# The last quantised product of a feed-forward block: magnitudes with a running maximum, and the signed product formed in the down stage

## What is computed

```python
def act_qdq(x):                       # one scale for the whole tensor
    scale = jnp.maximum(jnp.max(jnp.abs(x)) / 32767, 1e-12)
    return jnp.clip(jnp.round(x / scale), -32768, 32767) * scale
...
x = act_qdq(x)
up = act_qdq(x @ lpbq_dequant(w_up).T)
gate = act_qdq(x @ lpbq_dequant(w_gate).T)
sig = fixed_qdq_u16(jax.nn.sigmoid(gate))
gate = act_qdq(gate * sig)
o = act_qdq(gate * up)
return o @ lpbq_dequant(w_down).T
```

## Time and profile before

| | us |
|---|---|
| median of 3 runs (1158.4 to 1158.91) | 1158.68 |
| the profiled execution's own time | 1158.46 |
| its span in the trace | 1156.7 |
| last 74.7 us: product stage and its scale steps | 33.1 |
| down stage to the start of PE's second group | 8.95 |
| from there to the end | 32.65 |

### The profile page before, as it was taken

The page is one execution under the profiler, slowest core; times in us unless marked ns, Lnnn a source line. Parts: engine busy times, 40 slices in busy tenths (PEclk is TensorE's granted clock), DMA queues, the critical chain, the costliest instruction groups (busy, mean ns, idle before and its releaser), DMA issues.

```text
span 1156.7 us, 20436 instructions
## 1 busy us (share of the span) xinstructions
PE 1075.9 (93%) x8326; PEld 500.6 (43%) x8326; DVE 1006.6 (87%) x1390; ACT 604.5 (52%) x705; POOL 37.2 (3%) x41
## 2 busy tenths in 40 slices
PE   5999999999999999999999999999999998999059
PEld 3443344434443444344434443444343322887049
DVE  7687988898889889998999899987989999849995
ACT  3555555555555555545454555454555464449652
POOL 0500000000000000000000000000000000003200
PEclk9999999999999999999999999999999999999579
DMA  8001300010001000100010001000100000000002
GB/s 273 8 20 25 119 20 20 20 38 20 20 20 38 20 19 20 38 20 20 20 38 20 20 20 38 20 19 20 29 20 19 20 29 10 1 1 0 0 1 74
DMA packets 37860, 34.57 MB, mean 30 GB/s; under 512 B 14209, under 2 KB 28738, under 8 KB 37510
## 3 DMA queue, kind: packets, MB, share of 16 engines
q1 hardware_dynamic: 37766, 33.26, 9.3%
HBM read 30.75 MB, written 2.36 MB: 29 GB/s over the span
## 4 chain that ended last, share of the span: by engine, by line
PE 63%; DVE 24%; issue 6%; ACT 6%; DMA 0%; POOL 0%; POOLq 0%; DVEq 0%; ACTq 0%
PE ps L1345 20%; PE ps L1361 20%; DVE acc L906 9%; DVE e_buf L1000 6%; PE ps L1221 4%; PE ps L1273 3%; PE ps L1493 3%; PE ps L1231 3%; PE ps L1239 3%; PE ps L1538 3%; ACT e_buf L651 2%; PE ps L1250 1%; DVE gt L1148 1%; ACT z L732 1%; ACT z L734 1%
## 5 line engine op out<-in xcount | busy, mean ns | idle before, releaser
L651 ACT ACTIVATE e_buf<-ps 128x1024 f32<-128x1024 f32 x400 | 410.6, 1027 | 311.2 <-PE ps L1345 311.2
L1361 PE MATMUL ps<-e_buf,vb 64*64 64x512 f32 x3072 | 402.4, 594 | 7.0 <-DVE e_buf L1000 6.9
L906 DVE TENSOR_TENSOR acc<-acc,e_buf 128x1024 f32<-128x1024 f32 x320 | 388.8, 1215 | 0.0
L1000 DVE TENSOR_SCALAR e_buf<-e_buf 128x1024 f32<-128x1024 f32 x400 | 272.9, 682 | 71.3 <-ACT e_buf L651 70.1
L1361 PEld LDWEIGHTS ps<-e_buf,vb 64*64 64x64 f32 x3072 | 111.8, 133 | 225.7 <-issue 194.1
L1345 PE MATMUL ps<-qb,kb_odd 64*64 64x512 f32 x1600 | 208.7, 589 | 0.0
L1345 PE MATMUL ps<-qb,kb_even 64*64 64x512 f32 x1600 | 208.6, 589 | 0.0
L1345 PEld LDWEIGHTS ps<-qb,kb_odd 64*64 64x64 f32 x1600 | 61.6, 133 | 109.8 <-issue 109.5
L1345 PEld LDWEIGHTS ps<-qb,kb_even 64*64 64x64 f32 x1600 | 61.3, 133 | 110.2 <-issue 110.1
L1493 PE MATMUL ps<-hT,wgu 128*128 128x512 f32 x288 | 67.7, 396 | 0.1
L989 DVE TENSOR_TENSOR xacc<-ps,xacc 128x512 f32<-128x512 f32 x60 | 40.5, 687 | 27.2 <-PE ps L1273 26.7
(11 more groups left out here) (145 smaller groups left out, 770.9 us busy)
## 6 DMA issues: line engine op xcount, KB each, us to landing
ebc<-el_rows SPq DMA_DIRECT2D x64, 128.0 KB, 2.9
rden<-inv_rows SPq DMA_DIRECT2D x62, 128.0 KB, 2.9
xacc<-in_x_dram SPq DMA_DIRECT2D x4, 512.0 KB, 7.1
wst<-in_L_xattn_Wkv_dram SPq DMA_DIRECT2D x16, 128.0 KB, 2.8
out_dram<-z SPq DMA_DIRECT2D x7, 256.0 KB, 2.1
wst<-in_L_xattn_Wq_dram SPq DMA_DIRECT2D x8, 128.0 KB, 2.8
wo_raw<-in_L_xattn_Wo_dram SPq DMA_DIRECT2D x8, 128.0 KB, 2.9
acc<-in_ctx_dram SPq DMA_DIRECT2D x2, 512.0 KB, 7.2
```

The lines of the kernel that those rows point to most:

```text
L651: nc.scalar.activation(e_buf[:, g % E_BUFS, :, :], sc[:, g % 2, :, :], ACT.Exp, scale=float(DH) ** -0.5).then_inc(exp_done, 1)
L906: dve.tensor_tensor(acc[:, t0 % 3, :, :], a, e_buf[:, tiles_to(t0, st) % E_BUFS, :, :], ALU.add).then_inc(summed, 1)
L1000: dve.tensor_scalar(tile, tile, EXP_LO, EXP_HI, ALU.max, ALU.min).then_inc(clip_done, 1)
L1361: ins = pe.matmul(ps_o[DH * h:DH * h + DH, half, :], vb[rows, p % 2, st, DH * h:DH * h + DH], e_buf[rows, g % E_BUFS, h, :], start=(st == ...
```

## The change

For half of the chunks (`MAGS`: 2, 3, 6, 7, 10, 11) ACT writes the magnitudes of both rounded factors, and DVE multiplies them and keeps a running maximum in one instruction, `tensor_tensor_reduce`. For the other half (`SIGNED`: 0, 1, 4, 5, 8, 9) DVE multiplies the signed factors and reduces the product with `top` as before, now into and out of a scratch tile `om` that both kinds of chunk share, each step waiting for the one before. No product is kept: the down stage forms it again from the int16 factors, rounded in the same instruction (`scalar_tensor_tensor`). ACT makes the int16 gate of each group for that (`gate_integers`), and POOL makes all twelve chunks of the int16 `ui`, the six signed ones first. The gate integers have four buffers, and `ohl` moves into the memory of the gate and up weights. PE's program isn't touched.

```diff
--- before.py
+++ after.py
@@ -52,6 +52,10 @@
 FC = 2 * NB
 FCH = FT * N // FC
 GROUPS = NT // 2
+GQ_BUFS = 4
+MAGS = [e for e in range(FCH) if e % NBS >= 2]
+SIGNED = [e for e in range(FCH) if e % NBS < 2]
+POOL_UI = SIGNED + MAGS
 
 
 def rows_of(st):
@@ -278,14 +282,17 @@
                 hT = sb("hT", [P, 2, KT, N], F32R, stack=first)
                 up = sb("up", [P, FT, N], stack=first)
             ui = sb("ui", [P, FT, N], I16, stack=ffn)
-            sb("pad2", [P, (2 * KT * N - FT * N // 2)], stack=ffn)
-            ohl = sb("ohl", [P, 2, 2, FT, DM], F32R, stack=ffn)
             oi = sb("oi", [P, 2, FT, DM], I16, stack=ffn)
+            gs_i = sb("gs_i", [P, 2, FT, DM], I16, stack=ffn)
         zf = z[:, :, :].rearrange("p t d -> p (t d)")
         hi16 = zf[:, 0:N].bitcast(I16)
         sg = zf[:, 0:2 * FC].rearrange("p (a f n) -> p a f n", a=2, f=2)
         gi = zf[:, 2 * FC:3 * FC].bitcast(I16).rearrange("p (a f n) -> p a f n", a=2, f=2)
         su = zf[:, 3 * FC:4 * FC].bitcast(U16T).rearrange("p (a f n) -> p a f n", a=2, f=2)
+        gq = zf[:, 0:2 * FC].bitcast(I16).rearrange("p (a f n) -> p a f n", a=GQ_BUFS, f=2)
+        um = zf[:, 2 * FC:3 * FC].bitcast(I16).rearrange("p (a f n) -> p a f n", a=2, f=2)
+        om = zf[:, 3 * FC:4 * FC].rearrange("p (f n) -> p f n", f=2)
+        ohl = wgu[:, :, :, :, :].rearrange("p a b k f -> p (a b k f)").rearrange("p (a i f d) -> p a i f d", a=2, i=2, f=FT)
         wpiece = [zf[:, FF * n:FF * n + FF] for n in range(5)] + [wdown1[:, :]]
 
         psum = nc.psum_tensor("ps", [P, 8, NB], F32)
@@ -319,7 +326,8 @@
         scale_done = sem("scale_done")
         f1_ready, f1_out = sem("f1_ready"), sem("f1_out")
         gi_done, sig_done, su_done = sem("gi_done"), sem("sig_done"), sem("su_done")
-        gs_done, gq_done, ui_done, ui_pool, o_done = sem("gs_done"), sem("gq_done"), sem("ui_done"), sem("ui_pool"), sem("o_done")
+        gs_done, gq_done, ui_pool, o_written, o_done = sem("gs_done"), sem("gq_done"), sem("ui_pool"), sem("o_written"), sem("o_done")
+        um_done, gs_ready = sem("um_done"), sem("gs_ready")
         oi_done, o_high, o_low = sem("oi_done"), sem("o_high"), sem("o_low")
         f2_ready, f2_out, stored = sem("f2_ready"), sem("f2_out"), sem("stored")
 
@@ -367,10 +375,7 @@
 
         def await_ui(eng, e):
 
-            if e < 2:
-                eng.wait_ge(ui_pool, e + 1)
-            else:
-                eng.wait_ge(ui_done, e - 1)
+            eng.wait_ge(ui_pool, POOL_UI.index(e) + 1)
 
 
         @block.sync
@@ -540,7 +545,7 @@
                     pool.wait_ge(gs_done, e - 1)
                 pool.tensor_scalar(su[:, e % 2, :, :], sg[:, e % 2, :, :], U16, 1.0, ALU.mult, ALU.mult).then_inc(su_done, 1)
             pool.wait_ge(scale_done, 3)
-            for e in range(2):
+            for e in POOL_UI:
                 pool.tensor_scalar(chunk(ui, e), chunk(up, e), fsc[:, 2, 2:3], 1.0, ALU.mult, ALU.mult).then_inc(ui_pool, 1)
 
 
@@ -734,19 +739,34 @@
                 nc.scalar.activation(sg[:, e % 2, :, :], gi[:, e % 2, :, :], ACT.Sigmoid, scale=fsc[:, 1, 1:2]).then_inc(sig_done, 1)
             act.wait_ge(scale_done, 3)
             for e in range(FCH):
-                if e >= 2:
-                    nc.scalar.activation(chunk(ui, e), chunk(up, e), ACT.Copy, scale=fsc[:, 2, 2:3]).then_inc(ui_done, 1)
-                    act.wait_ge(o_done, e - 1)
-                nc.scalar.activation(gi[:, e % 2, :, :], chunk(gt, e), ACT.Copy, scale=fsc[:, 3, 2:3]).then_inc(gq_done, 1)
+                if e >= GQ_BUFS:
+                    act.wait_ge(o_done, e - GQ_BUFS + 1)
+                nc.scalar.activation(gq[:, e % GQ_BUFS, :, :], chunk(gt, e), ACT.Abs if e in MAGS else ACT.Copy,
+                                     scale=fsc[:, 3, 2:3]).then_inc(gq_done, 1)
+                if e in MAGS:
+                    nc.scalar.activation(um[:, e % 2, :, :], chunk(up, e), ACT.Abs, scale=fsc[:, 2, 2:3]).then_inc(um_done, 1)
+
+            def gate_integers(g):
+
+                if g >= 2:
+                    act.wait_ge(oi_done, g)
+                nc.scalar.activation(gs_i[:, g % 2, :, :], gt[:, :, DM * g:DM * g + DM], ACT.Copy, scale=fsc[:, 3, 2:3]).then_inc(gs_ready, 1)
+
+            act.wait_ge(ui_pool, len(SIGNED))
+            for g in range(2):
+                gate_integers(g)
             for m in range(2):
                 act.wait_ge(oi_done, m + 1)
                 nc.scalar.copy(ohl[:, 0, 0, :, P * m:P * m + P], oi[:, 0, :, P * m:P * m + P]).then_inc(o_high, 1)
+            gate_integers(2)
             for g in range(1, GROUPS):
                 act.wait_ge(oi_done, g + 2)
                 if g >= 2:
 
                     act.wait_ge(f2_ready, g - 1)
                 nc.scalar.copy(ohl[:, g % 2, 0, :, :], oi[:, g % 2, :, :]).then_inc(o_high, 1)
+                if g + 2 < GROUPS:
+                    gate_integers(g + 2)
 
 
         @block.vector
@@ -1142,15 +1162,23 @@
             link(top(fst[:, 3, pieces - 2:pieces], chunk(gt, FCH - 1)))
             scale_of(2, 2, pieces, 2)
             link(dve.tensor_tensor(pre[:, 4:5], fsc[:, 3, 1:2], fsc[:, 2, 1:2], ALU.mult))
+            dve.memset(fst[:, 4, :], 0.0)
             for e in range(FCH):
                 dve.wait_ge(gq_done, e + 1)
-                await_ui(dve, e)
-                dve.tensor_tensor(chunk(gt, e), gi[:, e % 2, :, :], chunk(ui, e), ALU.mult).then_inc(o_done, 1)
-                if e >= 1:
-                    dve.wait_ge(o_done, e)
-                    top(fst[:, 4, 2 * e - 2:2 * e], chunk(gt, e - 1))
+                if e in MAGS:
+                    dve.wait_ge(um_done, MAGS.index(e) + 1)
+                    if e:
+                        dve.wait_ge(o_done, e)
+                    dve.tensor_tensor_reduce(om, gq[:, e % GQ_BUFS, :, :], um[:, e % 2, :, :], 1.0, 0.0, ALU.mult, ALU.max,
+                                             fst[:, 4, 2 * e:2 * e + 1]).then_inc(o_done, 1)
+                else:
+                    await_ui(dve, e)
+                    if e:
+                        dve.wait_ge(o_done, e)
+                    dve.tensor_tensor(om, gq[:, e % GQ_BUFS, :, :], chunk(ui, e), ALU.mult).then_inc(o_written, 1)
+                    dve.wait_ge(o_written, SIGNED.index(e) + 1)
+                    top(fst[:, 4, 2 * e:2 * e + 2], om).then_inc(o_done, 1)
             dve.wait_ge(o_done, FCH)
-            link(top(fst[:, 4, pieces - 2:pieces], chunk(gt, FCH - 1)))
             scale_of(4, 1, pieces, 3)
             link(dve.tensor_tensor(fsc[:, 4, 3:4], fsc[:, 4, 1:2], tg[:, 1:2], ALU.mult))
 
@@ -1159,8 +1187,11 @@
 
                     dve.wait_ge(o_high, g)
                     dve.wait_ge(o_low, g - 1)
-                dve.tensor_scalar(oi[:, g % 2, :, r0:r1], gt[:, :, DM * g + r0:DM * g + r1], fsc[:, 4, 2:3], None,
-                                  ALU.mult).then_inc(oi_done, 1)
+                dve.wait_ge(gs_ready, g + 1)
+                if g == GROUPS // 2 and r0 == 0:
+                    dve.wait_ge(ui_pool, FCH)
+                dve.scalar_tensor_tensor(out=oi[:, g % 2, :, r0:r1], in0=gs_i[:, g % 2, :, r0:r1], scalar=fsc[:, 4, 2:3],
+                                         in1=ui[:, :, DM * g + r0:DM * g + r1], op0=ALU.mult, op1=ALU.mult).then_inc(oi_done, 1)
 
             def out_low(g):
                 dve.wait_ge(o_high, g + 2)
```

## The result

The changed kernel takes 1166.57 us (median of 4 runs, 1165.6 to 1167.08) against 1158.76 for the kernel before (4 runs). The ratio is 1.0066, 95% interval 1.0054 to 1.0078: 7.8 us slower. The forecast was slower, by 4.3 us; the upper end of its range, 1166.5, is 7.8 us above the 1158.68 that it started from, so the result lies just at that end.

A forecast was written before the change was run, and what follows sets the result against it. DVE was taken to bound the product stage and PE the down stage. Product stage -0.3, PE's queue +2.5 and down stage +2.2 made 4.4 us on 1158.46, giving 1163.0 us; range 1158.3 to 1166.5.

The forecast's parts named there:

- POOL's exclusion: Product stage: two-tensor DVE operations and POOL instructions exclude each other; 4.6 to 4.7 us waiting; rival without it 0.13.
- the two take turns: Product stage: DVE and POOL alternate when both always have work; a POOL that loses a turn moves 0.7 us.
- The fused maximum: Product stage, magnitude chunks: one `tensor_tensor_reduce` at 1.31 us, 1.35 with gap; dear rival 2.3 to 2.46, chance 0.14.
- PE's queue: Before the down stage: spreading matmuls queue behind nine idle matmuls that start later; adds 2.5 us.
- The rounding: Down stage: two-tensor int16 `scalar_tensor_tensor` takes 1.83 us for 1,536 columns, 1.01 for a half of group 0.
- the second mark: Spreading matmuls to PE's second down group: forecast 2.2 us longer, from the dearer rounding on DVE.
- The rule of half rate: Down stage rival: rounding with two non-bf16 SBUF sources at half rate, near 3.4 us; about 1175 us, chance 0.04.
- the old price: Down stage rival: rounding costs what the replaced operation did, so the stage adds 0; 1160.9 us, chance 0.09.
- ACT cost nothing: Product and down stages: ACT's passes, gate integers and `Abs` stay under DVE's or PE's time; no loss.
- the last term of the sum: From PE's second down group to the end: PE still sets the pace at 4.28 us a group; no further loss.
- the forecast's two steps: First product to spreading matmuls, +2.2 us; from there to PE's second down group, +2.2 us.
- the last mark: PE's second down group to the end of the span: forecast unchanged, 0 us more.

## Why the prediction was right, and what it missed

**POOL's exclusion** held. Seven two-tensor operations were expected to wait 4.6 to 4.7 us in all; the timeline gives 4.3 (each duration less 1.22). Taking POOL out gave 3.4 us, and POOL alone put into the kernel before cost 4.35. That the two take turns had rested on one place of the rows; that it held was in part luck.

**The fused maximum** was put at 1.35 us with its gap. It is 1.22 + 0.08, and a start every 1.36 to 1.41, with 0.14 to 0.18 us of wait ahead of each. Chunk 11 ends 28.25 us after the first product, where 27.7 was forecast; before it was 28.03. So DVE's list became 0.2 us longer and not 0.3 shorter.

**PE's queue** was the point that no edit names, and it held: the spreading matmuls start 2.65 us after the last chunk's end (2.9 forecast), and moving the idle matmuls alone took 2.3 us off.

**The rounding** was forecast at 1.83 us and is 1.81, and its halves at 1.01, which they are; the second mark grew by 2.3 where 2.2 was forecast. The rule of half rate that the prediction weighed, from the Trainium skill's Vector Engine (DVE) Microarchitecture Reference, "Points that are easy to get wrong", isn't borne out for two int16 sources, and the old price (1.01) isn't either. ACT cost nothing that can be seen, as said: the run with all its passes and the old rounding has the second mark at 8.88, the kernel before 8.65 and 8.96.

**What failed** is the last term of the sum, "nothing at the end", together with an item that the sum doesn't have: that the part ahead of the change takes the same time. With PE's first gap filled in both kernels the change costs 4.6 us in one group and 5.3 in the other, against the 4.4 of the sum; by the marks the forecast's two steps make 4.3 to 4.7 of it and the end, put at nothing, 0.5 to 0.8. The other 2.5 to 3.2 us of the 7.8 are PE's clock. The prediction had PE wait "some 2 us" before its second group and priced only the wait; in four of the six profiles with such an unfilled wait (1.9 us), PE then ran at the lower level for 3.4 us, which cost 1.5. In none of the eight other profiles, where that wait was 0.3 to 0.9 us, did it. At the turn from attention both kernels have the same gaps, and the fall after them took 3 to 14 us in the changed kernel and those derived from it, and 3 in the others. That the result still lies at the end of the range and not beyond it is luck: the range was wide for the price of the new instruction and for POOL's turns, and neither was off by much.

**What stays open.** Why the changed kernel had the longer fall in each of its three profiles (14, 7 and 7 us), and none of its 14 times below 1164.7, though its code there is the same, isn't shown. Derived kernels with the same gaps had it short (3 us in two of them). It was not the chip alone: on one chip, in one group, the changed kernel had 7 us and the kernel before 3. Second, the last mark at full clock is 33.1 to 33.2 us in every kernel derived from the changed one and 32.3 to 32.7 in the others; the 252 down matmuls take 30.5 us there, 29.95 or 29.7 here. The filled gap and the old rounding both leave it. It isn't a wait: in the traces one group of 36 follows the next every 4.32 us (120 ns a matmul) there and every 4.24 or 4.20 here, evenly, and so do the last groups, for which ACT makes no gate integers any more. The move of `ohl` into the weights' memory is a part of the change that all of these share; it wasn't tried alone, so this cause stays open.

## What to carry to other kernels

A pass moved to POOL isn't free because POOL is idle: a two-tensor operation of DVE waits for what is left of the POOL instruction that it meets, and ten more of 1.1 us cost this stage 3.4 (4.35 in the kernel before). When a producer's last steps get shorter, look at what fills another in-order queue ahead of the next hand-over: matmuls that were hidden by 4.5 us of DVE work stood in the way when only 1.3 were left. And an idle gap of PE can cost time behind it, where PE sets the time afterwards at a lower clock: eight idle matmuls in one gap of 2 us gave the kernel before 2.1 us and the changed one 4.6.

## What the runs showed of the hardware

- A two-tensor DVE operation and a POOL instruction wait for each other: products of 1.21 us took 2.02 to 2.10 beside POOL. By the durations, less what each takes alone, the second starts its work some 0.14 us before the first is recorded as ended. The Trainium skill, SBUF — State Buffer, "SBUF: two separate sides", says that a DVE operation with two SBUF inputs and a GpSimd operation that reads SBUF exclude each other; the experiments agree.
- A one-tensor reduction isn't touched: 1.21 us beside POOL and without. That doesn't hold for every one-tensor operation: the `TENSOR_SCALAR` behind POOL in the earlier trace rows took 0.97 us, and the same one at 972.67 us, with POOL idle, 0.68.
- A custom maximum over a product of 1,024 columns costs what the product costs (1.22 to 1.23 us), and the accumulator's read 0.08 more.
- In these profiles PE's granted clock fell to 0.5 at the waits of 1.9 to 2.1 us, in some executions and not in others, and at none of the waits of 0.3 to 0.9 us ahead of the second down group. It was back at 1.0 after 3 to 14 us, in the same code. After a long idle stretch nine idle matmuls took 3.63 to 4.21 us; at full clock ten took 2.40.
- Filling the first gap also made the times close: 1.0 and 1.3 us apart over 11 runs each, against 4.5 in the kernel before.
